# Handing over from attention to experts: a new order for the next layer's keys, the scatters, the zero rows and the tile table

## The reference

```python
# attention of layer L: 8 heads in layer 0, 16 in layer 1, 64 columns each
k = context @ W_k;  v = context @ W_v                 # 256 context rows x 192
out = softmax(q @ k.T * scale) @ v @ W_o + b_o        # layer 0 masks keys
# layer 0 experts: top 1 of 8, capacity 640 rows, the others pass through
idx = argmax(softmax(t @ Wr)); pos = cumsum(onehot) of the chosen expert
eout = relu(ein @ W1[e]) @ W2[e];  out = where(kept, eout, t) * factor
# layer 1 experts: top 2 of 8, no capacity
fused = silu(x @ W11[e]) * (x @ W12[e]);  y = fused @ W2[e]
out = sum of the two chosen experts' y, weighted
# each stage: x = x + stage(layernorm(x))
```

## Time and profile before

| | us |
|---|---|
| three runs, median | 1151.09 |
| lowest, highest | 1150.28, 1153.82 |
| the profiled execution's own time | 1155.69 |
| its span, first to last instruction | 1153.9 |

### The profile page before, as it was taken

The page is one execution under the profiler, slowest core; times in us unless marked ns, Lnnn a source line. Parts: engine busy times, 40 slices in busy tenths (PEclk is TensorE's granted clock), DMA queues, the critical chain, the costliest instruction groups (busy, mean ns, idle before and its releaser), DMA issues.

```text
span 1153.9 us, 25638 instructions
## 1 busy us (share of the span) xinstructions
PE 1045.8 (91%) x7860; PEld 974.7 (84%) x7860; DVE 734.3 (64%) x2257; ACT 672.7 (58%) x2490; POOL 520.0 (45%) x527
## 2 busy tenths in 40 slices
PE   6999997899999999889999999507999999989994
PEld 4688886799999999569999998507999999989994
DVE  6678886344444444766777776534677667767673
ACT  2688885544444443589999999304454454544541
POOL 1346776433333333346588886540333343333333
PEclk9899999899999999899999999858999999999997
DMA  9910001566666656101122221154837756497542
GB/s 323 338 39 19 34 29 69 192 229 225 226 233 220 228 195 198 56 19 38 38 74 72 74 71 57 63 202 156 241 61 235 237 127 180 67 340 241 129 63 29
DMA packets 91044, 163.52 MB, mean 142 GB/s; under 512 B 11858, under 2 KB 70100, under 8 KB 88532
## 3 DMA queue, kind: packets, MB, share of 16 engines
q1 hardware_dynamic: 72436, 133.27, 33.4%
q0 software_dynamic: 17376, 27.15, 11.3%
q10 hardware_dynamic: 1152, 2.13, 0.5%
HBM read 159.46 MB, written 63.34 MB: 193 GB/s over the span
## 4 chain that ended last, share of the span: by engine, by line
PE 77%; DVE 9%; DMA 6%; ACT 3%; issue 2%; POOL 1%; SPq 0%; DVEq 0%; ACTq 0%; POOLq 0%
PE psum L1408 14%; PE psum L674 11%; PE psum L659 11%; PE psum L1129 10%; PE psum L1146 10%; PE psum L1393 7%; DMA E_xin<-rows 5%; PE psum L631 4%; PE psum L376 2%; PE psum L340 2%; PE psum L680 2%; ACT L_prob L720 2%; PE psum L1381 2%; DVE L_m_lo L428 1%; PE psum L646 1%
## 5 line engine op out<-in xcount | busy, mean ns | idle before, releaser
L1527 POOL DMA_INDIRECT out<-E_y,E_dest x78 | 121.1, 1553 | 259.4 <-DVE E_y L1489 239.1
L720 ACT ACTIVATE L_prob<-psum,L_neg_max 128x64 f32<-128x64 f32 x768 | 228.6, 362 | 4.8 <-DVE L_neg_max L950 4.7
L1408 PE MATMUL psum<-E_xT_hi,E_up_w 128*128 128x256 f32 x1248 | 224.3, 279 | 2.9 <-DVE E_xT_lo L1468 2.9
L1408 PEld LDWEIGHTS psum<-E_xT_hi,E_up_w 128*128 128x128 f32 x1248 | 193.6, 190 | 3.5 <-DVE E_xT_lo L1468 3.5
L720 ACT ACTIVATION_READ_ACCUMULATOR L_prob<-psum,L_neg_max 128x1 f32 x768 | 195.4, 257 | 0.0
L1408 PE MATMUL psum<-E_xT_lo,E_up_w 128*128 128x256 f32 x624 | 174.0, 279 | 0.0
L1443 ACT ACTIVATE E_sg<-psum 128x256 f32<-128x256 f32 x156 | 59.9, 384 | 171.5 <-PE psum L1408 169.9
L1497 DVE TENSOR_TENSOR E_hf<-psum,E_sg 128x256 f32<-128x256 f32 x156 | 66.0, 423 | 89.8 <-ACT E_sg L1443 87.4
L1408 PEld LDWEIGHTS psum<-E_xT_lo,E_up_w 128*128 128x128 f32 x624 | 118.2, 189 | 0.0
L674 PE MATMUL psum<-L_n_hi,L_pT_hi 128*128 128x256 f32 x384 | 107.9, 281 | 10.9 <-DVE L_pT_lo L957 10.9
L752 POOL TENSOR_TENSOR L_prob<-L_prob,L_rcp 128x512 f32<-128x512 f32 (+1 forms) x64 | 94.3, 1473 | 42.9 <-DVE L_rcp L916 41.5
(11 more groups left out here) (201 smaller groups left out, 3090.6 us busy)
## 6 DMA issues: line engine op xcount, KB each, us to landing
E_up_w<-up SPq DMA_DIRECT2D x39, 2048.0 KB
E_w<-in_w SPq DMA_DIRECT2D x39, 512.0 KB
E_w<-in_w SPq DMA_DIRECT2D x16, 1024.0 KB, 7.8
E_xin<-rows SPq DMA_DIRECT2D x39, 260.0 KB
E_raw<-in_w SPq DMA_DIRECT2D x16, 512.0 KB, 6.7
up<-E_raw_hi SPq DMA_DIRECT2D x16, 512.0 KB, 5.9
up<-E_raw_lo SPq DMA_DIRECT2D x16, 512.0 KB, 3.9
rows<-zero SPq DMA_DIRECT2D x8, 640.0 KB, 14.4
```

Source lines behind the costliest of these rows:

```text
L720: last = e.activation(prob[q][:, h * KEYS:(h + 1) * KEYS], scores_ps(t)[:, h * KEYS:(h + 1) * KEYS], ACT.Exp, bias=nmx[:, q, h, :], accum_ ...
L1408: mm = q.matmul(bank, up_w[:, par, half, w, c, m * P:(m + 1) * P], x[:, c, :], start=(k == 0), stop=(k == 3 * KC - 1))
L1527: q.indirect_dma_start(p.out[:, :], bass.IndirectOffsetOnAxis(ap=dest[:, par, c, :], axis=0), y[:, par, c, :], None, compute_op=ALU.add).t ...
```

## The change

It has seven parts.

1. Five of the 16 key/value units of layer 1 are issued inside the last iterations of attention 0: two in iteration 32 and three in iteration 33, on PE before the rank matmuls and on ACT before the group's exponential. The other 11 stay where they were. They use banks 0 to 3 instead of 5 and 7. In experts 0 ACT copies them before it splits the down weights, not behind.
2. The scatters of tiles 20 and up go out earlier: from iteration 29 or 30 two tiles per iteration, behind the small POOL operations of the norm. In layer 1 tiles 20 to 31 form six groups of two instead of one of four per eight tiles, and `more` deals out twice as many steps from iteration 28.
3. DVE waits for layer 0's scatters to land before it makes the first low weights of experts 0.
4. The table: what doesn't depend on the routing is computed in iteration 2 (`plan_constants`); the rest is a chain of 13 steps with most operands in PSUM, and the experts' part is ready (semaphore at 2) before the first rows (3). Expert 0 gets at least one tile, so tile 0 is always its first.
5. Zero rows: ACT writes those of experts 0 to 4, SP those of 5 to 7. Expert 0's have their own semaphore.
6. SP loads the first weights of expert 0 behind the store of tile 29 (iteration 30 on DVE), and rows 0 to 255 as soon as the scatters and expert 0's zero rows have landed, without the table.
7. `vector_bias` is issued after unit group 2 of `tensor_m`'s low parts, not after group 3.

```diff
-    KV_BANKS = (0, 1, 2, 3) if layer == 0 else (5, 7)
+    KV_BANKS = (0, 1, 2, 3)
+    KV_AT = {NT: range(0, 2), NT + 1: range(2, 5)}
+    KV_AFTER = range(5, 2 * PR)
...
-        if i == 3:
+        if i == 2:
             vector_bias(e)
...
-    GROUPS = [(a, a + G) for a in range(0, NT - G, G)] + [(NT - 4, NT - 2), (NT - 2, NT)]
+    GROUPS = [(a, a + G) for a in range(0, NT - 4 - 4 * layer, G)] + [(a, a + 2) for a in range(NT - 4 - 4 * layer, NT, 2)]
...
-        return [u for u in range(NT - 4) if t == min(u + LAG, NT + 1)] + \
-            {NT + 2: [NT - 4, NT - 3], NT + 4: [NT - 2, NT - 1]}.get(t, [])
+        late = {NT - 2: (20, 21), NT - 1: (22, 23), NT + 1: (24, 25, 26, 27), NT + 2: (28, 29), NT + 4: (30, 31)} if layer == 0 \
+            else {NT - 3: (20, 21), NT - 2: (22, 23), NT - 1: (24, 25), NT + 1: (26, 27), NT + 2: (28, 29), NT + 4: (30, 31)}
+        return late[t] if t in late else [u for u in range(20) if t == u + LAG]
...
+                if t == NT - 3:
+                    first_weights(e)
...
+            if ahead and t in ahead.KV_AT:
+                ahead.tensor_kv(e, ahead.KV_AT[t])
             g = rank_at(t)
...
+            if ahead and t in ahead.KV_AT:
+                ahead.scalar_kv(e, ahead.KV_AT[t])
             for g, (a, b) in enumerate(GROUPS):
...
         q.tensor_copy(tail_i[:, :], p.next[:, 0, :]).then_inc(s_tab, 1)
-        c = Chain(q, s_tb, 0, 29)
...
+        need(q, s_exp, NT)
+        need(q, s_pc, 4 + 2 * TC)
+        c = Chain(q, s_tb, 0, 13)
+        c(q.tensor_tensor(t_a, p.next[:, 0, :], t_off[:, :], ALU.add))
+        c(q.tensor_scalar(t_b, t_a, 8, None, ALU.arith_shift_right))
+        q.tensor_copy(b0[:, 17:16 + E], b0[:, 9:8 + E].bitcast(I32))
+        c(q.tensor_scalar(b0[:, 16:17], b0[:, 8:9].bitcast(I32), 1.0, None, ALU.max))
...
+        q.tensor_tensor(p.tab[:, 2, 2:NT1], ra_p[:, 2:NT1], ra[:, 0:NT1 - 2, 0], ALU.not_equal).then_inc(s_tab, 1)
...
+        q.tensor_scalar(p.tab[:, 0, :], first[:, :, 0], float(IDLE_ROW), None, ALU.min).then_inc(s_tab, 1)
...
-                k = 2 * NR if t >= NT else k
+                k = 2 * NR if t >= NT else 2 * k if t >= NT - 4 and layer == 1 else k
...
         split_w1(0, 0)
+        kv(q)
         split_w2(0, 0)
-        kv(q)
         split_x(0)
...
+        rows_from.rows_landed(q)
         split_w(0, 0)
...
+    def first_weights(q):
+
+        rows_from.need(q, rows_from.s_sim, NT)
+        q.dma_start(up_w[:, 0, :, :, :, :].rearrange("p j w c f -> p (j w c f)").bitcast(F32), up_d[0, :, :]).then_inc(s_w[0], 16)
+        q.dma_start(w2[:, 0, :, :], w2_d[:, 0, :, :]).then_inc(s_w2[0], 16)
...
+        rows_from.rows_landed(q)
+        q.wait_ge(rows_from.s_tail0, 16)
+        q.dma_start(xin[:, 0, :, :], d1[0:T1, :].rearrange("(c p) d -> p c d", p=P)).then_inc(s_x[0], 16)
         q.wait_ge(rows_from.s_tab, 2)
-        rows_from.need(q, rows_from.s_sim, NT)
-        load_up(0, 0)
-        load_w2(0, 0)
-        rows_from.rows_landed(q)
-        load_x(0, 0)
+        load_up(1, 1)
+        load_w2(1, 1)
+        rows_from.tails_landed(q)
+        q.wait_ge(rows_from.s_tab, 3)
+        load_x(1, 1)
...
-            att1.tails(e)
+            att1.tails(e, range(0, 5))
```

More of the change, by code:

```diff
@@ L328, in gpsimd, with tensor_kv @@
             e.wait_ge(before.s_stlo, 16 * 2 * E)
-    def tensor_kv(e, before_rows=None):
-        need(e, s_w, 32)
-        if layer == 1:
-            before_rows.need(e, before_rows.s_xfTc, NT)
-        for j in range(2 * PR):
+    def tensor_kv(e, units):
+        for j in units:
+            if j == 0:
+                need(e, s_w, 32)
             if j == PR:
@@ L341, in tensor_kv, with scalar_kv @@
             mm.then_inc(s_kv, 1)
-        need(e, s_kvc, 2 * PR)
-    def scalar_kv(e):
-        for j in range(2 * PR):
+            if j == 2 * PR - 1:
+                need(e, s_kvc, 2 * PR)
+    def scalar_kv(e, units):
+        for j in units:
             need(e, s_kv, j + 1)
@@ L508, in attention @@
         rowf = small("rowf", [P, G, CH])
-        tiles = small("tiles", [P, 1, E])
-        tiles_a = small("tiles_a", [P, 1, E])
-        tiles_i = small("tiles_i", [P, 1, E], I32)
-        cmp = small("cmp", [P, NT1, E])
         num = small("num", [P, NT1, 1])
         num_i = small("num_i", [P, NT1], I32)
-        base_row = small("base", [P, 1, E])
-        first = small("first", [P, NT1, 1])
-        ra, rb = (small(x, [P, NT1, 1]) for x in ("ra", "rb"))
+        num_t = small("num_t", [P, NT1])
+        t_off = small("t_off", [P, E])
+        upto = small("upto", [P, E, E])
+        room = small("room", [P, E])
+        first, ra = (small(x, [P, NT1, 1]) for x in ("first", "ra"))
         tail_i = small("tail_i", [P, E], I32)
@@ L520, in attention @@
         zero = at(160, "zero", [P, TC * DW])
-        s_num, s_tb, s_tab, s_tail, s_zero = (p.sem(n + x) for x in ("number", "table_steps", "table", "tails_zeroed", "zero"))
+        s_num, s_pc, s_tb, s_tab, s_tail0, s_tail, s_zero = (
+            p.sem(n + x) for x in ("number", "plan_constants", "table_steps", "table", "tail0_zeroed", "tails_zeroed", "zero"))
         got = at(64, "got", [P, G, D])
@@ L592, in sync, with tails @@
                 e.dma_start(out_t[:, t, :], p.x[:, t, 0:D]).then_inc(s_store[t % 4], 16)
-    def tails(e):
+                if t == NT - 3:
+                    first_weights(e)
+    def tails(e, experts):
         need(e, s_zero, 1)
         need(e, s_tab, 1)
-        for j in range(E):
+        for j in experts:
             r = e.value_load(tail_i[0:1, j:j + 1], min_val=0, max_val=IDLE_ROW - T1)
-            e.dma_start(p.d1[bass.ds(r, T1), :].rearrange("(p c) d -> p (c d)", p=P), zero[:, :]).then_inc(s_tail, 16)
+            e.dma_start(p.d1[bass.ds(r, T1), :].rearrange("(p c) d -> p (c d)", p=P), zero[:, :]).then_inc(s_tail if j else s_tail0, 16)
     def rows_landed(e):
@@ L605, in rows_landed, with tails_landed @@
             need(e, s_scat[r], 16 * CH * len(range(r, NT, RING)))
[L606 to L607 removed]
+    def tails_landed(e):
+        need(e, s_tail, 16 * (E - 1))
     def x_stored(e):
@@ L611, in x_stored, with tensor @@
             need(e, s_store[j], 16 * NT // 4)
-    def tensor(e):
+    def tensor(e, ahead=None):
         e.wait_ge(p.s_sel, 3)
@@ L693, in tensor, with scalar @@
                 mm.then_inc(s_pos, 1)
-    def scalar(e):
+    def scalar(e, ahead=None):
         for t in iters:
@@ new lines, in plan_constants @@
+    def plan_constants(q):
+        need(q, s_num, 1)
+        q.tensor_copy(num[:, :, 0], num_i[:, :]).then_inc(s_pc, 1)
+        need(q, s_pc, 1)
+        q.tensor_scalar(num_t[:, :], num[:, :, 0], float(T1), None, ALU.mult).then_inc(s_pc, 1)
+        q.tensor_scalar(t_off[:, :], p.expert8[:, 0, :], -float(ROOM), float(T1 - 1), ALU.mult, ALU.add).then_inc(s_pc, 1)
+        q.tensor_tensor(upto[:, :, :], p.expert8[:, :, :].to_broadcast([P, E, E]),
+                        p.expert8[:, :, :].rearrange("p o e -> p e o").to_broadcast([P, E, E]), ALU.is_le).then_inc(s_pc, 1)
+        for r in range(TC):
+            q.tensor_scalar(p.spare[:, r, :], p.token[:, r:r + 1], float(TOK), None, ALU.add).then_inc(s_pc, 1)
+            q.tensor_scalar(p.shift[:, r, :], p.token[:, r:r + 1], -1.0, float(T1), ALU.mult, ALU.add).then_inc(s_pc, 1)
@@ L909, in vector @@
                 setup.vector_n(e, t + 4)
-            if t == 1 and layer == 1:
+            if t == 2 and layer == 1:
                 e.memset(zero[:, :], 0.0).then_inc(s_zero, 1)
+                plan_constants(e)
             if ok(t + 1):
@@ L1568, in _ @@
             setup1.late_loads(e)
-            att1.sync(e)
+            att1.sync(e, exp1.first_weights)
+            att1.tails(e, range(5, E))
             exp1.sync(e)
@@ L1573, in _ @@
         def _(e):
-            setup0.tensor_kv(e)
-            att0.tensor(e)
-            setup1.tensor_kv(e, att0)
+            setup0.tensor_kv(e, range(8))
+            att0.tensor(e, setup1)
+            setup1.tensor_kv(e, setup1.KV_AFTER)
             exp0.tensor(e)
```

74 lines of the change are left out of this document (30 added, 44 removed).

## The result

| | before | changed |
|---|---|---|
| median of the runs, us | 1150.80 (4 runs) | 1137.06 (4 runs) |
| lowest, highest | 1150.28, 1153.82 | 1133.49, 1139.87 |
| profiled execution, its span | 1155.69, 1153.9 | 1133.49, 1131.7 |

A forecast was written before the change was run, and what follows sets the result against it. PE, busy 91% of the span, was taken as the bound, so only shorter PE holes count: 1.7 + 2.0 + 5.5 + 1.1 + 0 + 17.8 = 28.1 us off 1155.7, less 4.6 and rounded, gives 1123.5 us; range 1115 to 1135.

The forecast's parts named there:

- First handover: Attention 0 to experts 0: the rows' split starts earlier, gain 5.5 us, bounds 6.5 down to -0.7.
- Five units move into the waits: First handover: five of 16 key/value units fit into PE's waits for the rank matmuls, leaving 11 behind.
- 11 x 0.86: First handover: the 11 remaining key/value units take 9.5 us at ACT's full-clock pitch, from about 205.2 to 214.7.
- ACT is late next: First handover: ACT, free at 217.0, then sets the start of the rows' split, 1.2 us behind the rows at 215.8.
- rival (c): First handover: moved keys run at 1.2 GHz and hold up the ranks, so no gain: 1129 to 1131 us; 6 in 100.
- Second handover: Attention 1 to experts 1: fewer scatters left, rows loaded without the table, first up matmul at 767; gain 17.8 us.
- SP's issue 1.76 later as in layer 0: Second handover: SP issues the row load 1.76 us after the last scatter's end at 760.0, so at 761.8.
- the cover that the prediction counted on: Last iterations of layer 1: DVE's doubled steps fit gaps where it waits for PE and ACT; 0 us, lower bound -3.
- The 4.6 us between profile and median: Whole kernel: profiled execution 1155.69 us, median 1151.09; the 4.6 difference was subtracted at the end of the sum.
- rival (b): Layer 1's start and experts 1's first tile keep 2.4 GHz, 2.4 + 3 us more gain: 1118 us; 13 in 100.
- Rival (d): Loop of experts 1: longer waits for rows at about eight expert changes eat the gain, up to 1155 us; 4 in 100.
- Start and start of layer 1: Setup and layer 1's start: earlier bias shortens PE's waits, gaining 1.7 + 2.0 us (2.0 from clock) and 1.1 us.

The follow-up runs named there:

- e1_again: The changed kernel, unaltered, run and profiled a second time; median 1141.92 us.
- e2_keys_back: The changed kernel with all 16 key and value units behind attention 0 again, none early; 1142.75 us against 1141.92.
- e6: The changed kernel with two early key units, the down weights' split behind the rows' split, SP's three zero-row blocks behind the first rows' load; 1141.41 us.
- e8: As e6, but with no early key units, all 16 behind attention 0; 1143.95 us.
- e12: As e11, plus SP's three zero-row blocks behind the loads of the first rows and tile 1's weights, in front of tile 1's rows; 1144.49 us.
- e4: The changed kernel with only expert 0's zero rows written beside the last scatters, those of experts 1 to 7 after they landed; 1144.85 us against 1141.92.
- e15: The changed kernel with the first handover and the bias as in the kernel before; ratio to the kernel before 0.9861.
- e13: The kernel before with one edit, the bias's two operations one group earlier (part 7 alone); ratio to the kernel before 0.9955.
- e11: The changed kernel with two early key units instead of five and the down weights' split behind the rows' split; 1138.78 us.
- e5_before_again: The kernel before, unaltered, run again for a second profile; median 1149.31 us.
- e3: The changed kernel with ACT's split of expert 0's down weights behind the split of the rows; 1140.31 us against 1141.92.
- e14: The changed kernel with all of the first handover as before (keys, layer 0's scatters, split order, DVE's first step); ratio to the kernel before 0.9837.

## Why the prediction was wrong

The signs of most of the sum and its largest term were right, the path of the second handover too. Of the 28.1 us, 13 were not there in the mean of four profiles each. The steps that failed:

1. **First handover, 5.5 forecast, -1.6 measured: 7.1 us.** "Five units move into the waits", "11 x 0.86" and "ACT is late next" failed, because all of it was priced at full clock. Of the range that the prediction itself gave, 6.5 to -0.7, I took the upper part; what came lies below its lower end. In the mean the rows' split begins only 1.1 us earlier than before, counted from the last logits, which is 4.4 of the 7.1. Three units took 4.52 us in front of the rank matmuls, which came 1.75 us later (3.1 in e1_again), and the eleven behind took 11.4 us. The next 2.4 is a term that I put at nothing: the way from the rows' split to the first down matmul, 16.3 us before and 17.6 to 19.1 changed, because the up matmuls ran in part or wholly at half clock (15.4 to 16.9 us instead of 14.1). The last 0.3 lies ahead of the last logits. This is my rival (c), to which I gave 6 in 100, and somewhat more than it.

   What the variants show and what not: the place of the down weights' split makes PE's wait 2.54 us in all seven profiles that have it in the middle and 1.38 in the other thirteen. Behind 2.54 the up matmuls kept full clock in one of seven (e2_keys_back), behind 1.38 in eleven of thirteen. With no early units the handover takes 49.76 with the split in the middle, 47.59 late and 48.40 in front. With two early units and the late split it takes 46.89 to 47.44, with five 49.57; but the latter is one profile, of the kind in which the ranks came 3.1 us late and not 1.75, so that the three units cost 2.4 us is shown for this kind alone. The 0.4 that two units bring over none rests on a single profile of none.
2. **Second handover, 17.8 forecast, 13.4 measured: 4.4 us.** 1.2 is the reference: I priced the gain from one profile, whose handover took 53.86, and one of four takes 49.16. The other 3.2 are terms that were sized too small, counted from the last logits in the mean of four: the first of the twelve scatters starts 2.7 us later than before and not 1.7 (0.9 at their end); "SP's issue 1.76 later as in layer 0" is 3.5 (1.8); from the load to the up matmul it takes 6.3 and not 5.4 (0.9); 0.4 came back, most of it the 0.3 that I had left as a margin. The latency was taken from a place where no zero rows are written. Here it grows with the blocks beside it: from the start of the last scatter until SP's wait for them ends it takes 4.3 to 4.6 us in the four profiles in which all eight blocks are out by then, 3.2 and 3.4 with ACT's five (e6, e8), 2.9 with four (e12), 2.5 with one (e4). Where SP or ACT load the row numbers slowly, the last blocks go out 3 to 4 us behind that start instead, SP's load is issued at 3.8 to 4.3, and takes up to 2.2 us longer. e4, e6, e8 and e12 show that the same traffic, moved behind the first rows, makes tile 1 late. That it had to go somewhere I should have seen: I placed tile 1's weights and rows in time, 3 us before they were needed, and gave the zero rows no place in that sum.
3. **Attention 1, 0 forecast, -2.0 measured; its end -0.7.** I looked for added instructions there, and put both at nothing. What differs in attention 1 is the clock behind a wait of 2.72 us: it takes 231.4 to 231.8 us in the eight profiles without half clock there, 233.9 to 234.3 with 6.8 us of it and 234.7 to 235.1 with 10.2. Full clock was kept in five of five profiles in which neither the bias nor the first handover is changed (four of before, e15), and in 3 of 15 in which either is, a grouping that I made after I saw them. The second half of the change isn't needed for the long case (e13) and doesn't bring it by itself (e15, one profile). That the first half acts by where it leaves the program in time is argued, not shown; e11 and e12, alike up to there, differ. And none of the slower executions of the kernel before was profiled. The end of attention 1 took 33.1 to 34.2 us in the five profiles with its order as before, and 33.1 to 36.7 in the fifteen others, over 34.2 in eleven. From the logits of iteration 30 to those of 31 it takes 8.3 to 10.1 us in these eleven, 8.1 in e5_before_again and 6.7 to 6.9 in the rest. PE waited no longer there, 11.5 to 12.9 us from iteration 25 on in ten of the eleven against 12.6 before (14.1 in e3), so the cover that the prediction counted on held; what is more is time at half clock. Whether the change brings that or chance, these counts don't settle.
4. **The 4.6 us between profile and median.** I carried them over as a constant. The fastest of the four profiles of before is 6.3 us shorter than the one that I priced from, 2.2 of them in the start and 4.7 in the second handover, which is what the change removes; if the 4.6 lay there too, subtracting them again counted part of the gain twice. The executions at the median have no profile, so this is argued. Together with the fast profiled execution of after it is why the two first profiles differ by 22 us, while the ratios give gains of 11.5 to 20. (1127.6 less 4.6 is also 1123.0, not 1123.5.)

Of rival (b), more clock came back at the start of layer 1 in two of four profiles, and none in the first tile of experts 1, whose 48 up matmuls took 8.71 us in the changed kernel and 8.22 before. Rival (d) rested on 48.1 us of waits in the loop of experts 1, of which 31.0 are the second hole and the rest counts PE and its weight loads; a loop in which PE waits 7.8 us could still have become slower, but it gained 1.0.

Start and start of layer 1 were right in mechanism and size (4.8 forecast, 4.6 measured). At the start of layer 1 PE's wait was 2.27 us, 2.3 forecast; its gain was 1.1 to 1.2 us in two profiles and 2.1 in the two others, which had 3.4 us at half clock instead of 6.8. Right as well were the small routing steps and table constants, the number of scatters left, the wait for rows ahead of tile 1, and that no scatter of layer 0 took 2.6 us any more once DVE's low part stood behind the landing (1.08 at most in the changed kernel; 2.59 before, 2.60 in e14 and e15, where it stands as before).

## What to carry to other kernels

Work that is moved into waits of PE costs what it takes at the clock of those waits, and what stands behind it in PE's order can be late by it: here two units in front of the rank matmuls left them where they were, three more moved them by 1.75 to 3.1 us. Price what follows a handover at both clocks, too. A landing latency holds for queues as full as where it was read, and from the point it was read from, the start or the end of the transfer's instruction; list the bytes that other engines write at the moment the critical transfer lands. Before a sum is made from one profiled execution whose time is some us above the median, find in which stretch those us lie; if it is the stretch the change removes, the gain may be smaller by them.

## What the runs showed of the hardware

- After the same wait of PE (2.72 and 2.73 us), ten matmuls ran in 2.76 or 3.71 us, in two executions of the same kernel. The half clock went with an earlier, small shift of the program: 5 of 5 profiles kept the clock in one group, 3 of 15 in the other.
- Behind a wait of 2.54 us the up matmuls of experts 0 kept full clock in 1 of 7 profiles, behind one of 1.38 us in 11 of 13.
- Register loads on SP and ACT beside indirect scatters took 0.7 us a step in some executions and not in others of the same kernel; ACT's eight blocks took 9.1 or 16 to 16.3 us.
- From the start of the last indirect scatter to the end of SP's wait for them it took 4.3 to 4.6 us with eight blocks of 260 KB written beside them, 3.2 and 3.4 with five, 2.9 with four, 2.5 with one, and 8.4 beside eight blocks and 2.5 MB of weights.
- The executions of the kernel before spread by 11 to 17 us within each later set (1149.7 to 1164.9 in one), three to five times the 3.5 us of the first; its medians differed by 11 us from set to set.
